# A sequence convolution with expert layers: the first tile of each pass stored whole behind its last addition, in place of two halves of 64 channels

## The chip, the core and the metric

One core of one Trainium2 chip runs the whole program. The metric is the device time of one launch in microseconds (us). Times of engines and transfers come from one execution that the hardware profiler recorded.

## The reference, cut to what matters

```python
# x: (8, 4096, 512) float32; T = 4096 tokens; 8 experts of rank 64, 2 per token
x = x + L0_attn(layernorm(x))      # a convolution along the sequence, for each channel
x = x + L0_ffn(layernorm(x))       # low-rank experts; y is added for the first 4096 rows only

def L0_attn(x, ...):               # 16 decaying states per channel make the kernel k
    ...
    out = irfft(rfft(xt, n=2 * l) * rfft(k, n=2 * l))[..., :l]
    return swapaxes(out) + x * omega
```

Input and output are 64 MiB each. The tokens of sequence 0 are the ones that the experts treat between the two halves of the convolution.

## The kernel before, in words

The 8 sequences are handled in two passes (g = 0 and 1) of four sequences each. A pass holds 128 positions on the partitions and 128 rows (4 sequences x 32 chunks) beside each other, and goes over the 512 channels in DG = 4 tiles of 128 channels. Tiles are numbered t = 0 to 3 in pass 0 and 4 to 7 in pass 1. A tile is computed in BT = 8 blocks of 16 channels, each block in two units of 8 channels, so UT = 16 units per tile. Between the passes the tokens go through the experts.

The buffer `xb` has two halves, each the size of one tile (128 partitions x 128 rows x 128 channels, 8 MiB). Tile t is computed in place in one half: GpSimd (POOL, L625) and VectorE (DVE, L1342) subtract the mean from a unit's 8 channels, DVE multiplies (L1353), TensorE (PE) convolves (L1562, L1575, L1587), and DVE adds the result back into `xb` (L1364), which counts the semaphore `s_ev` up by one per unit. The other half of `xb` is meanwhile emptied of tile t-1 and filled with tile t+1.

All these transfers are issued by the queue of SyncE (SP), in an order written out by hand in `tile(g, t, first, final)`. A tile is moved in PIECES = 16 pieces of PR = 8 rows. A whole piece is 512 KB: 1024 runs of 512 bytes (128 channels). A half piece (`store_part` with 64 channels) is 256 KB: 1024 runs of 256 bytes. In HBM the runs lie 2048 bytes apart. For each of the 8 blocks the queue first issues the tap and decay tables of the block three ahead (`load_weights`, L787 and L791, 256 and 128 KB, which wait for ACT and POOL to be done with the buffers), then some four or five pieces.

What it issues in the pass's tiles (they are called first, second, third and fourth below):

- In the first tile: 16 loads of the second tile into the other half (L732), then, from block 4 on and after `s_ev` has reached half of the tile's units, 16 half stores of the tile itself, channels 0 to 63 (L851, counted by `s_early`).
- In the second tile: a wait until all units of the first are added (`s_ev` >= 16 t); 16 half stores of the first tile's channels 64 to 127 (L851, `s_put[j]`), and 16 loads of the third tile (L732). Load j goes into the rows that store j has emptied and waits for `s_put[j]`. `in_turn` (LAG is 4) orders them: four stores, then load and store by turns (12 of each), then the last four loads.
- In the third tile: the same order, but with 16 whole stores (`store_tile`, L749) and the loads of the fourth tile.
- In the fourth tile: 16 whole stores of the third; then half stores of the fourth's first 64 channels, and the other 64 after its last unit.

DVE and POOL begin a tile only when all of its 16 pieces have landed (`wait(..., s_x, loads_in(...))`). The second tile of a pass is ready long before and its first blocks overlap the last of the first tile (`joined(t)`); at the other borders DVE first makes the last additions of the tile and then takes the next.

```python
            def in_turn(n):
                m = n - LAG
                if not 0 <= m < 2 * (PIECES - LAG):
                    return n
                return LAG + m // 2 if m % 2 else PIECES + m // 2
```

Of the kernel before, what the change touches and what calls it, by code (L numbers as in the profile page):

```python
# [20 lines left out]
P = 128  # L21
# [6 lines left out]
def wait(eng, sem, value):  # L28

    if isinstance(value, int) and value <= 0:  # L30
        return
    eng.wait_ge(sem, value)
# [16 lines left out]
def build(nc, x, delta, alpha, beta, gamma, omega, ew, ei, w1a, w1b, w2a, w2b, out, ei_experts=8):  # L49
# [5 lines left out]
    DG = D // P  # L55
# [3 lines left out]
    UT = P // UC  # L59
# [3 lines left out]
    BT = UT // 2  # L63
# [10 lines left out]
    PIECES = 16  # L74
    PR = P // PIECES
    YP = CH // PR
# [36 lines left out]
    with ctx:  # L113
# [3 lines left out]
        def sem(name):  # L117
            return ctx.enter_context(nc.semaphore(name))
# [172 lines left out]
        s_ev = sem("s_ev")  # L291
        s_early = sem("s_early")
        s_put = [sem(f"s_put{k}") for k in range(PIECES)]
# [140 lines left out]
        def _(pool):  # L434
# [263 lines left out]
                    scatter(q - 2, (q - 2) % 4)  # L698

            pool.wait_ge(s_sf, 4)  # L700
            pool.wait_ge(s_early, 16 * (PIECES + YP))
            for j in range(YP):
                pool.wait_ge(s_put[j], 16 * DG)
            pool.wait_ge(s_yz, 16)
# [15 lines left out]
        def _(sp):  # L720
            def piece(g, t, j, per=PR):

                v = ((t + g) % 2) * P + j * per, g * P + j * per, (t % DG) * P
                return [a if isinstance(a, int) else sp.snap(a) for a in v]

            def load_tile(g, t, pieces, stored=None, per=PR):

                for j in pieces:
                    r0, row, d0 = piece(g, t, j, per)
                    if stored is not None:  # L730
                        wait(sp, s_put[j], 16 * stored(j))
                    sp.dma_start(xb_row[:, bass.ds(r0, per), :], x_rows[:, bass.ds(row, per), bass.ds(d0, P)])\  # L732
                      .then_inc(s_x, 16)
# [3 lines left out]
            def stored(g, t):  # L737

                return lambda j: t + 1 if g == 0 or j < YP else t

            def store_tile(g, t, pieces):

                for j in pieces:
                    r0, row, d0 = piece(g, t, j)
                    if g == 0 and j < YP:
                        dst = y_rows[:, j * PR:(j + 1) * PR, bass.ds(d0, P)]
                    else:
                        dst = o_rows[:, bass.ds(row, PR), bass.ds(d0, P)]
                    sp.dma_start(dst, xb_row[:, bass.ds(r0, PR), :]).then_inc(s_put[j], 16)  # L749
# [27 lines left out]
            def load_weights(i, k):  # L777

                kb = i % NK if isinstance(i, int) else sp.snap(i % NK)
                row = taps_d[bass.ds(kb, 1)].rearrange("k s i d -> k (s i d)")  # L780
                dec = decay_d[bass.ds(kb, 1)].rearrange("k s n d -> (k s) (n d)")
                turned, placed = 2 * (i - WB + 1), i - WB + 1
                now(sp, turned, placed)
                wait(sp, s_rev, turned)

                src = bass.AP(row.tensor, row.offset, [[2, ZR], [2 * (P + ZR), SB], [1, 2 * P]])
                sp.dma_start(taps_in[k * ZR:(k + 1) * ZR], src).then_inc(s_w[k], 16)  # L787
                wait(sp, s_wd, placed)
                if isinstance(i, int) and NK <= i < NK + WB:
                    sp.wait_ge(s_dn, grp(NP))  # L790
                sp.dma_start(dk[:, k, :], dec).then_inc(s_dk[k], 16)  # L791
# [6 lines that stand above are left out]
                return LAG + m // 2 if m % 2 else PIECES + m // 2  # L798

            def tile(g, t, first, final):  # L800
                second = t == g * DG + 1
                for b in range(BT):
                    if not (first and b == 0) and not (final and b + WB > BT):
                        load_weights(t * BT + b + WB - 1, (b + WB - 1) % WB)
                    if b == 0 and not first:
                        wait(sp, s_ev, UT * t)

                    paced = b - 1 if first else b
                    for n in range(2 * PIECES * paced // (BT - 1), 2 * PIECES * (paced + 1) // (BT - 1)):
                        j = n if first or final else in_turn(n)  # L810
                        if first and 0 <= j < PIECES:
                            load_tile(g, t + 1, [j])
                        elif first and b >= BT // 2 and PIECES <= j < 2 * PIECES:
                            if j == PIECES:
                                sp.wait_ge(s_ev, UT * t + UT // 2)
                            store_part(g, t, j - PIECES, slice(0, P // 2), s_early)
                        elif second and 0 <= j < PIECES:
                            store_part(g, t - 1, j, slice(P // 2, P), s_put[j])
                        elif not first and 0 <= j < PIECES:
                            store_tile(g, t - 1, [j])  # L820
                        elif PIECES <= j < 2 * PIECES and not first and not final:
                            if second and j == PIECES:
                                sp.wait_ge(s_early, 16 * (PIECES if g == 0 else 2 * PIECES + YP))
                            load_tile(g, t + 1, [j - PIECES], stored(g, t - 1))
                    if final and g == 0 and b >= BT // 2:
                        if b == BT // 2:
                            for j in range(PIECES):
                                sp.wait_ge(s_put[j], 16 * t)
                            for k in range(SQ):
                                sp.wait_ge(s_scat[k], 16 * (NSEND // SQ))  # L830
                            sp.dma_start(slots_l, slot_d.rearrange("(c p) w -> c p w", p=P)).then_inc(s_slots, 16)
                            sp.dma_start(load1a, w1a.rearrange("(m p) d -> p m d", p=P)).then_inc(s_wl1, 16)
                            for j in range(KC):
                                sp.dma_start(load2a[:, j, :], w2a[j * P:(j + 1) * P, :]).then_inc(s_wl, 16)
                            store_early(g, t, range(YP))
                        elif b < BT - 1:
                            copy_out(b - BT // 2)
                    if final and g == 1 and b == BT - 1:
                        store_early(g, t, range(PIECES))

            def store_early(g, t, pieces):

                sp.wait_ge(s_ev, UT * t + UT // 2)
                for j in pieces:
                    store_part(g, t, j, slice(0, P // 2), s_early)

            def store_part(g, t, j, cols, done):

                r0, row, d0 = piece(g, t, j)
                rows = y_rows[:, j * PR:(j + 1) * PR, :] if g == 0 and j < YP else o_rows[:, row:row + PR, :]  # L850
                sp.dma_start(rows[:, :, d0 + cols.start:d0 + cols.stop], xb_row[:, r0:r0 + PR, cols]).then_inc(done, 16)  # L851

            def copy_out(j):

                rows = slice(j * (T // 4), (j + 1) * (T // 4))
                sp.dma_start(o_tok[rows, 0:(DG - 1) * P], y_d[rows, 0:(DG - 1) * P]).then_inc(s_copy, 16)

            def tiles(g):
                t0 = g * DG
                if g == 0:  # L860
                    for k in range(1, WB):
                        load_weights(k, k)
                tile(g, t0, True, False)
                for t in range(t0 + 1, t0 + DG - 1):
                    tile(g, t, False, False)
                tile(g, t0 + DG - 1, False, True)
# [55 lines left out]
            sp.wait_ge(s_ev, UT * NT)  # L922
            for j in range(PIECES):
                store_part(1, NT - 1, j, slice(P // 2, P), s_put[j])
            sp.wait_ge(s_early, 16 * (YP + 3 * PIECES))
            for k in range(2):
                sp.wait_ge(s_s[2 * k], 16 * ((NQ + 1 - k) // 2))
                sp.wait_ge(s_s[2 * k + 1], 16 * (NP // 2))
# [862 lines left out]
```

## Time and profile before

| | |
|---|---|
| time, median of 3 runs | 1080.95 us (1079.19 to 1082.27) |
| the profiled execution's own time | 1070.18 us |
| its span, first to last instruction | 1068.0 us |
| PE busy | 869.4 us (81%) |
| DVE busy | 816.4 us (76%) |
| ACT busy | 761.4 us (71%) |
| POOL busy | 571.5 us (54%) |
| bytes moved | 286.11 MB, mean 268 GB/s |
| pass 0, first tile to the fourth's last addition | about 117 to 375 us |
| pass 1, the same | about 790 to 1046 us |

The profiled execution ran 10.8 us under the median of the three timed runs and 2.2 us over its span; sums made on the trace are made against 1070.18 and then laid onto 1080.95. Busy shares are means over stages with different limits. DMA shares are the packet times of the 16 DMA engines in a stretch; where transfers overlap within an engine they can exceed 1. A time written beside a transfer on the SP queue is that of its issue: when the queues behind it are full, an issue takes long.

### The profile page before, as it was taken

Reading aid. Unit: us, or ns where it says so; the run is one execution under the profiler, and the core shown is the slowest. Engines: PE = TensorE matmul, PEld = TensorE weight load, DVE = VectorE, ACT = ScalarE, POOL = GpSimd, SP = SyncE. Lnnn points to the kernel's source line nnn. Section 1 sums busy time; section 2 is a strip of 40 time slices with the busy share of each in tenths; the row PEclk is TensorE's granted clock in tenths of the full one; section 3 lists DMA queues with packets and bytes.
Section 4 is the critical chain, followed back from the end, with each engine's and each line's share of the span. In section 5 each row is a group of like instructions: output and inputs, shape, how many; then the busy total and the mean of one; then the engine's idle time right before and its main releaser. Section 6 shows DMA issues by size and latency. Waiting matters only on the chain.

```text
span 1068.0 us, 31991 instructions
## 1 busy us (share of the span) xinstructions
PE 869.4 (81%) x11186; PEld 730.9 (68%) x11186; DVE 816.4 (76%) x1350; ACT 761.4 (71%) x1124; POOL 571.5 (54%) x641
## 2 busy tenths in 40 slices
PE   2770588887868969999999999997878889786981
PEld 1550477776757758888888888886757777675771
DVE  7988899987969834577777777775689998797891
ACT  3882599997969756566665665664459999696990
POOL 5444788867857232666666656655553333332330
PEclk9995699998989979999999999999989999898996
DMA  8999899999999979999999999899669999999977
GB/s 300 351 400 385 211 264 209 271 266 295 308 279 285 327 182 309 257 293 318 286 312 259 242 268 244 246 256 240 174 157 268 226 252 281 287 296 300 295 159 158
DMA packets 390529, 286.11 MB, mean 268 GB/s; under 512 B 124784, under 2 KB 338434, under 8 KB 389948
## 3 DMA queue, kind: packets, MB, share of 16 engines
q1 hardware_dynamic: 345980, 211.67, 72.6%
q0 software_dynamic: 17952, 34.42, 14.6%
q10 hardware_dynamic: 26528, 39.14, 10.4%
q8 instruction: 39, 0.64, 0.3%
q14 instruction: 30, 0.25, 0.1%
HBM read 195.57 MB, written 98.77 MB: 276 GB/s over the span
## 4 chain that ended last, share of the span: by engine, by line
PE 31%; issue 17%; ACT 15%; DVE 14%; DMA 13%; POOL 3%; SPq 2%; DVEq 1%; ACTq 1%; POOLq 0%
PE ps L1688 8%; DMA xb<-L_attn_x 6%; PE ps L1714 6%; ACT wb L1032 6%; DVE xb L1364 4%; ACT wb L1038 4%; PE ps L1562 4%; PE ps L1575 3%; PE ps L1587 3%; DMA wide<-y_d,slot_g 3%; ACT carry L1008 3%; DVE wb L1182 2%; PE ps L1650 2%; PE ps L1663 2%; DVE state L1380 2%
## 5 line engine op out<-in xcount | busy, mean ns | idle before, releaser
L1575 PE MATMUL ps<-xn,wb 128*128 128x128 f32 x2048 | 273.0, 288 | 0.0
L1575 PEld LDWEIGHTS ps<-xn,wb 128*128 128x128 f32 x2048 | 248.0, 198 | 17.0 <-issue 2.3
L625 POOL TENSOR_TENSOR cen<-xb,mean 128x512 f32<-128x512 f32 x128 | 142.8, 1119 | 217.0 <-DVE state L1380 144.2
L1353 DVE TENSOR_TENSOR xn<-cen,rstd 128x1024 f32<-128x1024 f32 x128 | 177.1, 1384 | 44.9 <-POOL cen L625 36.1
L1140 ACT ACTIVATE cen<-ps 128x1024 f32<-128x1024 f32 x110 | 109.2, 1023 | 101.6 <-PE ps L1688 64.7
L1562 PE MATMUL ps<-xn,near 128*32 128x128 f32 x2048 | 87.5, 291 | 113.0 <-DVE xn L1353 67.9
L1364 DVE TENSOR_TENSOR xb<-xb,ps 128x1024 f32 (+1 forms) x128 | 152.7, 1193 | 7.6 <-PE ps L1587 7.6
L1031 ACT ACTIVATE wb<-wide 32x1024 f32<-32x1024 f32 x126 | 144.5, 1147 | 15.4 <-DMA wide<-taps_d 12.9
L1562 PEld LDWEIGHTS ps<-xn,near 128*32 128x32 f32 x2048 | 52.6, 113 | 137.2 <-issue 72.1
L1688 PE MATMUL ps<-carry,wb 64*128 64x256 f32 x1024 | 126.8, 388 | 7.7 <-DVE carry L1426 4.6
L1688 PEld LDWEIGHTS ps<-carry,wb 64*128 64x128 f32 x1024 | 99.4, 190 | 37.1 <-issue 18.5
L1195 DVE BATCH_NORM_STATS2 xb<-xb 128x512 f32 (+1 forms) x128 | 84.3, 684 | 45.3 <-DMA xb<-L_attn_x 45.1
L1032 ACT ACTIVATE wb<-wide 32x768 f32<-32x768 f32 x126 | 114.8, 911 | 1.5
L505 POOL DMA_INDIRECT slot_d<-rowf,posi x64 | 106.1, 1658 | 11.9 <-issue 11.9
L1342 DVE TENSOR_TENSOR cen<-xb,mean 128x512 f32<-128x512 f32 x128 | 90.2, 705 | 9.3 <-DMA xb<-L_attn_x 9.2
L1714 PE MATMUL ps<-cen,xn 128*64 128x128 f32 x1536 | 96.4, 275 | 0.0
L1587 PE MATMUL ps<-state,carry 32*128 32x128 f32 x2048 | 93.6, 297 | 0.0
L1182 DVE BATCH_NORM_STATS2 wb<-xb 128x512 f32 (+1 forms) x128 | 79.8, 681 | 15.7 <-DMA xb<-L_attn_x 14.5
L1714 PEld LDWEIGHTS ps<-cen,xn 128*64 128x64 f32 x1536 | 84.3, 137 | 5.3 <-issue 5.1
L1587 PEld LDWEIGHTS ps<-state,carry 32*128 32x128 f32 x2048 | 69.2, 186 | 25.9 <-issue 25.1
L1038 ACT ACTIVATE wb<-wb 64x512 f32<-64x512 f32 x128 | 80.5, 629 | 4.9 <-DVE wb L1466 1.8
L1008 ACT ACTIVATE carry<-far,rate 128x384 f32<-128x384 f32 x128 | 79.0, 617 | 3.2
(211 smaller groups left out, 1311.4 us busy)
## 6 DMA issues: line engine op xcount, KB each, us to landing
xb<-L_attn_x SPq DMA_DIRECT2D x160, 512.0 KB, 7.4
out<-xb SPq DMA_DIRECT2D x72, 512.0 KB, 6.4
xb<-L_attn_x ACTq DMA_DIRECT2D x128, 256.0 KB, 5.8
out<-xb SPq DMA_DIRECT2D x88, 256.0 KB, 4.7
wb<-L_ffn_w_B SPq DMA_DIRECT2D x78, 256.0 KB
wide<-taps_d SPq DMA_DIRECT2D x63, 256.0 KB, 5.8
dk<-decay_d SPq DMA_DIRECT2D x63, 128.0 KB, 5.6
out<-y_d SPq DMA_DIRECT2D x4, 1536.0 KB, 11.6
```

The source lines that it names most:

```text
L625: pool.tensor_tensor(cen[:, k, 0:QB // 2].rearrange("p b r d -> p r b d"), unit_view(pool, g, i, k)[:, :, 0:UC // 2] .rearrange("p r (b d) ...
L1008: act.activation(carry[:, k, 0:CR + P], far[:], ACT.Exp, scale=rate[:, bass.ds(col, 1)])\
L1031: act.activation(dst[0:ZR], src, ACT.Copy)
L1032: act.activation(dst[ZR:2 * ZR, :, :, ZR:P], src[:, :, :, 0:P - ZR], ACT.Copy).then_inc(s_rev, 1)
L1038: act.activation(taps[2 * ZR:P, :, :, 2 * ZR:P], taps[0:2 * ZR, :, :, 0:2 * ZR], ACT.Copy)\
L1353: dve.tensor_tensor(xn[:, k].rearrange("p (b d) r -> p b d r", d=2), cen[:, k].rearrange("p b r d -> p b d r"), rstd[:, g * P:(g + 1) * P] ...
L1364: dve.tensor_tensor(view, view, ps[:, QB * k:QB * k + QB, 0:2 * P] .rearrange("p b (d r) -> p r b d", d=2), ALU.add).then_inc(s_ev, 1)
L1562: ins = pe.matmul(ps[b * 2 * N:(b + 1) * 2 * N, QB * k, 2 * P:3 * P], near[:, h, k * QB + b, d:d + 2, :].rearrange("p z n -> p (z n)"), xn ...
L1575: ins = pe.matmul(ps[:, QB * k + b, d * P:(d + 1) * P], wb[:, h, k * QB + b, d, :], xn[:, k, 2 * b + d, :], start=(b > 0 and d == 0), stop ...
L1587: ins = pe.matmul(ps[:, QB * k + b, d * P:(d + 1) * P], carry[rows, k, d * P:(d + 1) * P], state[rows, k, :], start=False, stop=True, skip ...
L1688: ins = pe.matmul(ps[:, 2 * (b % 2) + h, f * QT:(f + 1) * QT].rearrange("p (a t) -> p a t", a=2), w1bs[half_rows, k, c * P:(c + 1) * P], r ...
L1714: ins = pe.matmul(ps[h * RANK:(h + 1) * RANK, 4, 0:P], w2as[:, (f // 2) * (FC // 2) + 2 * b + f % 2, :], act_at(q, b)[:, f, side * P:(side ...
```

## The change

The first tile of a pass is no longer stored in two halves. Its 16 half stores in its own second half are dropped; in the second tile of the pass `store_tile` stores it whole, piece by piece, in the places of the order that the second halves had. The two waits that belonged to the early halves go, and the counts of `s_early` elsewhere follow. Loads, their order, all computation and the third and fourth tiles of each pass stay.

```diff
-            pool.wait_ge(s_early, 16 * (PIECES + YP))
+            pool.wait_ge(s_early, 16 * YP)
...
             def tile(g, t, first, final):
-                second = t == g * DG + 1
...
                         if first and 0 <= j < PIECES:
                             load_tile(g, t + 1, [j])
-                        elif first and b >= BT // 2 and PIECES <= j < 2 * PIECES:
-                            if j == PIECES:
-                                sp.wait_ge(s_ev, UT * t + UT // 2)
-                            store_part(g, t, j - PIECES, slice(0, P // 2), s_early)
-                        elif second and 0 <= j < PIECES:
-                            store_part(g, t - 1, j, slice(P // 2, P), s_put[j])
                         elif not first and 0 <= j < PIECES:
                             store_tile(g, t - 1, [j])
                         elif PIECES <= j < 2 * PIECES and not first and not final:
-                            if second and j == PIECES:
-                                sp.wait_ge(s_early, 16 * (PIECES if g == 0 else 2 * PIECES + YP))
                             load_tile(g, t + 1, [j - PIECES], stored(g, t - 1))
...
-            sp.wait_ge(s_early, 16 * (YP + 3 * PIECES))
+            sp.wait_ge(s_early, 16 * (YP + PIECES))
```

## Rows read from the trace of the kernel before

**Rows 1.** The page's strip of DMA busy tenths in 40 slices.
```profile
DMA  8999899999999979999999999899669999999977
```
**Rows 2.** Timeline at the border from second to third tile, both passes: start, us, instruction, [idle].
```profile
238.26 1.22 DVE L1364 TENSOR_TENSOR xb<-xb,ps 128x1024 f32<-128x1024 f32 x1 [1.28 <-PE ps L1587]
...
242.30 1.59 POOL L625 TENSOR_TENSOR cen<-xb,mean 128x512 f32<-128x512 f32 x1 [9.67 <-DMA xb<-L_attn_x]
...
913.29 2.65 POOL L625 TENSOR_TENSOR cen<-xb,mean 128x512 f32<-128x512 f32 x2 [9.41 <-DMA xb<-L_attn_x]
```
**Rows 3.** Timeline of SP's queue in the second tile, passes 0 and 1: start, us, issues.
```profile
182.39 2.92 SPq L851 DMA_DIRECT2D y_d<-xb  x4
...
187.79 0.42 SPq L732 DMA_DIRECT2D xb<-L_attn_x  x1
...
229.32 6.67 SPq L732 DMA_DIRECT2D xb<-L_attn_x  x4
...
238.94 0.45 SPq L791 DMA_DIRECT2D dk<-decay_d  x1
...
855.02 2.94 SPq L851 DMA_DIRECT2D out<-xb  x4
...
860.34 0.40 SPq L732 DMA_DIRECT2D xb<-L_attn_x  x1
...
900.13 5.99 SPq L732 DMA_DIRECT2D xb<-L_attn_x  x4
...
909.51 1.64 SPq L791 DMA_DIRECT2D dk<-decay_d  x1
```
**Rows 4.** The same timeline in the third tile, passes 0 and 1.
```profile
249.06 0.45 SPq L732 DMA_DIRECT2D xb<-L_attn_x  x1
...
294.52 8.04 SPq L732 DMA_DIRECT2D xb<-L_attn_x  x4
...
911.90 5.39 SPq L749 DMA_DIRECT2D out<-xb  x4
...
919.76 0.48 SPq L732 DMA_DIRECT2D xb<-L_attn_x  x1
...
966.27 7.13 SPq L732 DMA_DIRECT2D xb<-L_attn_x  x4
```
**Rows 5.** DMA view of four stretches: 182:236, 239:302, 855:905 and 912:972.
```profile
DMA packets 33957, 13.83 MB, mean 256 GB/s; under 512 B 17496, under 2 KB 33956, under 8 KB 33956
...
DMA packets 35150, 19.00 MB, mean 302 GB/s; under 512 B 1221, under 2 KB 35147, under 8 KB 35147
...
DMA packets 32755, 13.43 MB, mean 269 GB/s; under 512 B 17038, under 2 KB 32754, under 8 KB 32754
...
DMA packets 33091, 18.00 MB, mean 300 GB/s; under 512 B 693, under 2 KB 33089, under 8 KB 33089
```
**Rows 6.** Timeline of SP's queue: the stores in the first tile, and in the fourth.
```profile
152.80 3.35 SPq L851 DMA_DIRECT2D y_d<-xb  x2
...
177.97 0.67 SPq L791 DMA_DIRECT2D dk<-decay_d  x1
...
307.32 6.29 SPq L749 DMA_DIRECT2D y_d<-xb  x4
...
340.24 0.82 SPq L791 DMA_DIRECT2D dk<-decay_d  x1
```
**Rows 7.** Timeline of DVE: the eighth and the sixteenth addition of pass 0's first tile.
```profile
151.58 1.18 DVE L1364 TENSOR_TENSOR xb<-xb,ps 128x1024 f32 x1
...
181.18 1.19 DVE L1364 TENSOR_TENSOR xb<-xb,ps 128x1024 f32<-128x1024 f32 x1
```
**Rows 8.** Waits in 117:182 (total, times, longest us); then the chain: start, us, what.
```profile
PE ps L1562 <- DVE xn L1353: 38.6, 1, 38.6
...
119.81 3.71 PE ps L1575 x16
...
246.44 3.71 PE ps L1575 x16
```

## The prediction, as put on record before the changed kernel ran

> **What bounds the kernel now.** I read the page's strips first. The DMA engines are busy nine tenths or more in nearly every slice [rows 1], so it is not enough to ask which engine computes longest; one has to ask at each border between tiles whether the data or the computation comes last. The view that answers this is the timeline around a border. At the end of the second tile of pass 0, DVE makes its last addition from 238.26 to 239.48 us and could take the next tile at once; POOL had been idle for 9.67 us and begins the third tile at 242.30, released by a load of `x`. In pass 1 it is the same, at 913.29 after 9.41 us [rows 2]. So the third tile starts when the last of its 16 pieces lands, in both passes. The reader should see that a microsecond more in the transfers ahead of this point moves everything behind it by a microsecond.
>
> Next the timeline of SP's queue in that stretch, to see what sets the landing. The second tile's stream begins at 182.39 with the first half store (the last addition of the first tile has just come in) and its last four loads are issued from 229.32 to 235.99: 53.6 us for 16 half stores, 16 loads and the tables. In pass 1 it goes from 855.02 to 906.12, 51.1 us [rows 3]. Four issues take 2.9 us at the start, four loads 6 to 6.7 us at the end: the queues are full by then and the issue waits for the DMA engines. The stream is bound by the transfers, not by the order's waits.
>
> **What is removed from the first tile: nothing on the path.** 16 half stores per pass go from the second half of the first tile. What the computation could gain there is bounded by the pitch of the additions. From the eighth to the sixteenth, 151.58 to 181.18, eight units take 29.6 us, 3.70 each, with the half stores running [rows 7]. From there to the last addition of the second tile, 238.26, are 16 units in 57.1 us, 3.57 each, the last two of them short because no next unit is staged between them [rows 2, 7]. Even if the whole difference were owed to the stores it would be 8 x 0.13 = 1.0 us. I take 0. The dropped work can't be used for anything else there: the second tile is already loaded and the third needs the rows that the first still occupies. The wait for `s_early` at the first load of the second tile goes too; by the rows those halves were issued by 178 us, and the load behind that wait was issued at 187.79 [rows 3, 6], so it cost nothing. The waits at the pass's end cost nothing either, as they count stores from 200 us earlier. No computing instruction is added, and the number of packets falls.
>
> **What is added to the second tile: 16 x 256 KB = 4.19 MB per pass, ahead of the last load.** In each of the 16 places a whole store stands where a half stood. The trace has the whole form next door, in the third tile, in the same order with the same neighbours. Four ways to price 16 whole in place of 16 half stores:
>
> 1. The alternating part alone, 12 loads and 12 stores with five pairs of tables. Pass 0: 229.32 - 187.79 = 41.5 us with halves, 294.52 - 249.06 = 45.5 whole, so 3.9 us for 12 and 5.2 for 16. Pass 1: 900.13 - 860.34 = 39.8 and 966.27 - 919.76 = 46.5, so 6.7 for 12 and 9.0 for 16 [rows 3, 4].
> 2. Bytes over rate. In pass 0 the second tile moves 13.83 MB at 256 GB/s in 54 us and the third runs at 302 GB/s. With 4.19 MB more and that rate: 18.02 / 0.302 = 59.7 us, so 5.7 more. In pass 1: 17.62 MB at 300 GB/s is 58.7 us against 50, so 8.7 more [rows 5].
> 3. Stores without loads beside them, each with four pairs of tables. The first tile's 16 halves run from 152.80 to 178.64, 25.8 us; the fourth tile's 16 whole from 307.32 to 341.06, 33.7 us. Difference 7.9 [rows 6].
> 4. The whole stream, from first store to last load issued. Pass 1: 51.1 us in the second tile, 973.4 - 911.90 = 61.5 in the third, so 10.4 more [rows 3, 4]. This is too much by the backlog that the third tile inherits: its first four stores take 5.39 us to issue where the second tile's take 2.94, because the loads before them are still under way, while the second tile starts with empty queues. I keep it as the upper end.
>
> The values lie between 5.2 and 10.4 us. For pass 0 I take 7, between the 5.2 to 5.7 of its own rows and the 7.9 of the store-only rows; for pass 1, where its own rows say 8.7 and 9.0, I take 8.5.
>
> The Trainium skill (DMA: Bandwidth & Descriptors, Specifications) asks for 512 bytes or more per run for line rate and says that below that the engine does a read-modify-write. It would favour this change, which turns 256-byte runs into 512-byte ones. The trace agrees only in part: a half store is dearer than half a whole one, but not as dear as a whole one.
>
> **Whether anything absorbs it.** In pass 0 the tables behind the loads are issued by 239.39 and the third tile's first store goes out at 239.51, just when the last addition of the second tile (239.48) allows it [rows 2, 3]. With the stream 7 us later, SP comes to that wait 7 us after it is met, so the third tile's stream is late by the same amount as its computation. In pass 1 SP was done at 911.15 and waited 0.75 us for the last addition [rows 3, 4]; that wait disappears, so I give back 0.5. The third tile ends in the same race, which the loads won't win better than before, since both sides moved together. The fourth has nothing to load, its computation sets its end, and it starts later by the whole delay. PE's clock: PE waits longer at the border, and the first group behind such a wait costs 3.71 us at the lower clock; but it costs 3.71 us behind the 38.6 us of idle time at the pass's start as well as behind the present gap [rows 8], so a longer gap adds nothing. What is late next is thus the start of the third tile, the fourth, the experts behind pass 0, and the end.
>
> **Sum.** 0 from the first tile, +7.0 in pass 0, +8.5 - 0.5 in pass 1: +15.0 us. The profiled execution took 1070.18 us, so its like would take 1085.2. The profiled execution is 10.8 us below the median of the timed runs; the delay doesn't depend on what makes that difference, so I add it to the median: 1080.95 + 15 = 1096 us.
>
> **Rivals.**
> A, the delay is as long as the third tile's stream says, 10.4 in each pass, because the first loads now also wait for whole stores to land. For it: the order is the third tile's to the letter. Against it: the queues are empty at 182 and 855 us. +20.8 us: 1102.
> B, no change. By the skill's rule on runs under 512 bytes, taken to the letter, a half store would cost the DMA engines as much as a whole one; as a mechanism of this kernel, the time would go by runs and not by bytes. For it: both streams have about the same number of packets (33,957 and 35,150, 32,755 and 33,091) [rows 5]. Against it: the times for them differ, 25.8 against 33.7 us in the store-only stretches [rows 6]. It gives 0: 1081.
> C, faster. The short runs are what slows the loads beside them, and whole stores let the loads go so much quicker that the stream becomes shorter. The rate does rise, from 256 to 302 and from 269 to 300 GB/s. The point that decides: the rate must reach 18.02 MB / 54 us = 334 GB/s in pass 0 and 17.62 / 50 = 352 in pass 1 for no loss; no stretch of the third tile holds more than 302 on the mean [rows 5]. If the stream then came early enough to end the loads at the last addition, it would save the 242.30 - 239.48 = 2.8 us of pass 0 and, in pass 1, the about 1.4 us from the last addition (SP's first store of 911.90 shows it) to 913.29: 1080.95 - 4.2 = 1077 [rows 2, 4]. The 1 us of the first tile, in two passes 2, would add to it.
> D, half the delay: the cheap 5.2 us of pass 0 in both passes and the 1 us gain of the first tile twice: +8.4, 1089.
>
> **How the numbers follow.** My forecast, 1096 with its own span of 1092 to 1100, has 0.66; A 0.10, D 0.13, B 0.07, C 0.04. The range reaches from D to A, 1089 to 1102, and leaves B, C and a little beyond A outside. A measurement of this kernel can tell about 0.3% from no change, 3.2 us. Forecast, A and D are slower by more: 0.89; B is the same, 0.07; C is faster, 0.04.
>
> **What the profile after would show.** Right: no stores on SP's queue in the first tile, the additions there still 3.7 us apart; in the second tile L749 in place of L851, the last four loads issued up to some 243 us in pass 0 and 59 to 60 us after the stream's start in pass 1; POOL's wait for the load at that border 16 to 18 us in place of 9.7 and 9.4; a rate of about 300 GB/s there; and the third and fourth tiles as long as before. Wrong: a rate near 340 GB/s in the second tile (towards B or C), a pitch in the first tile under 3.6 us, or a third tile that gains back what the second lost. A pass 0 with much less delay than pass 1 would mean that the alternating part, my first price, was the right one by itself.

## The result and the profile after

The changed kernel takes 1092.09 us (median of 4 runs, 1088.57 to 1095.47) against 1080.33 us for the kernel before (4 runs, 1079.19 to 1082.27). The ratio is 1.0119, with a 95% interval of 1.0090 to 1.0148: 1.2% slower. The profiled execution spans 1089.6 us, its own time is 1091.77.

The page's summary and the totals of the DMA engines, after:

```profile
span 1089.6 us, 31957 instructions
...
DMA  8999994999999989999999999999679299999976
...
DMA packets 357249, 286.11 MB, mean 263 GB/s; under 512 B 58736, under 2 KB 305154, under 8 KB 356668
```

The same 286.11 MB now travel in 33,280 packets fewer (the page before had 390,529), and two dips (the 4 and the 2) have come into the DMA strip where it had nines [rows 1]. They are the second halves of the two first tiles, which have lost their stores. The DMA engines have less to do in all, and the kernel is slower.

The timeline of SP's queue in pass 0's and pass 1's second tile (start, us, issues) answers to [rows 3]:

```profile
181.47 3.91 SPq L749 DMA_DIRECT2D y_d<-xb  x4
...
188.69 0.65 SPq L732 DMA_DIRECT2D xb<-L_attn_x  x1
...
234.61 7.45 SPq L732 DMA_DIRECT2D xb<-L_attn_x  x4
...
245.25 7.96 SPq L749 DMA_DIRECT2D y_d<-xb  x4
...
868.96 3.98 SPq L749 DMA_DIRECT2D out<-xb  x4
...
921.67 7.59 SPq L732 DMA_DIRECT2D xb<-L_attn_x  x4
```

From the first store to the last issued load it is now 242.06 - 181.47 = 60.6 us in pass 0 (53.6 before) and 929.26 - 868.96 = 60.3 in pass 1 (51.1 before). What comes of it is seen at the border to the third tile, the point at which the third tile's last load has landed and POOL begins to compute it. The timelines of DVE and POOL answer to [rows 2]:

```profile
237.38 1.22 DVE L1355 TENSOR_TENSOR xb<-xb,ps 128x1024 f32<-128x1024 f32 x1 [1.21 <-PE ps L1578]
248.41 0.69 DVE L1333 TENSOR_TENSOR cen<-xb,mean 128x512 f32<-128x512 f32 x1 [9.81 <-DMA xb<-L_attn_x]
...
248.47 1.59 POOL L625 TENSOR_TENSOR cen<-xb,mean 128x512 f32<-128x512 f32 x1 [16.72 <-DMA xb<-L_attn_x]
...
935.95 2.65 POOL L625 TENSOR_TENSOR cen<-xb,mean 128x512 f32<-128x512 f32 x2 [18.10 <-DMA xb<-L_attn_x]
```

POOL waits 16.72 and 18.10 us where it waited 9.67 and 9.41: 7.1 and 8.7 us more, and for the same loads. The DMA view of 181:242 and 869:929 shows the added bytes and the rate, beside [rows 5]:

```profile
DMA packets 33923, 18.02 MB, mean 295 GB/s; under 512 B 1109, under 2 KB 33921, under 8 KB 33921
DMA packets 33514, 18.03 MB, mean 301 GB/s; under 512 B 662, under 2 KB 33511, under 8 KB 33511
```

The second tile now looks like the third did: its packets are as many as before, its bytes 18.0 in place of 13.8 and 13.4 MB, and the rate 295 to 301 GB/s. The first tile has not become quicker. Its eighth and its sixteenth addition, beside [rows 7]:

```profile
150.65 1.19 DVE L1355 TENSOR_TENSOR xb<-xb,ps 128x1024 f32 x1
...
180.26 1.19 DVE L1355 TENSOR_TENSOR xb<-xb,ps 128x1024 f32<-128x1024 f32 x1
```

29.6 us for eight units, as before.

**Where the 21.6 us between the two profiles are.** The spans differ by more than the medians (11.8 us), so I divide them at DVE's first multiplication of a pass and the end of its last addition. Pass 0 takes 257.6 us before and 263.8 after, pass 1 257.1 and 264.7: +6.2 and +7.6, together 13.7. Between the passes, where the two kernels do the same, the experts take 414.8 us before and 423.6 after, +8.8; start and end make -0.9. The experts' stretch is 413 to 430 us long among all executions profiled here. On one chip it took 423.2 us in the changed kernel (e8) and 415.8 and 416.2 in two kernels with the same late stores (e9, e10), so I take its 8.8 us for scatter. That the change has no part in it is not shown. For everything below, the lengths of the two passes are therefore read beside the times.

### The profile page after: what moved, and what is told of

Same layout as the page of the kernel before. It is cut to its first block, busy times and chain, and to the rows that moved or that the text cites. A ratio compares the mean times of both kernels' runs of the same rounds, so it can differ in the third digit from the quotient of the medians.

```text
span 1089.6 us, 31957 instructions
## 1 busy us (share of the span) xinstructions
PE 875.3 (80%) x11186; PEld 731.7 (67%) x11186; DVE 813.4 (75%) x1350; ACT 761.7 (70%) x1124; POOL 570.6 (52%) x641
## 2 busy tenths in 40 slices
DMA packets 357249, 286.11 MB, mean 263 GB/s; under 512 B 58736, under 2 KB 305154, under 8 KB 356668
## 4 chain that ended last, share of the span: by engine, by line
PE 37%; issue 16%; ACT 14%; DVE 12%; DMA 8%; SPq 6%; POOL 2%; ACTq 1%; DVEq 1%; POOLq 0%
PE ps L1679 10%; PE ps L1705 10%; ACT wb L1023 5%; DMA xb<-L_attn_x 4%; ACT wb L1029 4%; DVE xb L1355 4%; PE ps L1654 3%; PE ps L1641 3%; PE ps L1553 3%; SPq L732 3%; DVE wb L1173 2%; ACT carry L999 2%; PE ps L1721 2%; SPq L749 2%; PE ps L1578 2%
## 5 line engine op out<-in xcount | busy, mean ns | idle before, releaser
L1566 PE MATMUL ps<-xn,wb 128*128 128x128 f32 x2048 | 271.7, 288 | 0.0
L1566 PEld LDWEIGHTS ps<-xn,wb 128*128 128x128 f32 x2048 | 247.0, 197 | 17.0 <-issue 2.3
L1131 ACT ACTIVATE cen<-ps 128x1024 f32<-128x1024 f32 x110 | 109.5, 1024 | 93.4 <-PE ps L1679 53.7
L505 POOL DMA_INDIRECT slot_d<-rowf,posi x64 | 106.3, 1661 | 11.8 <-issue 11.7
L1705 PE MATMUL ps<-cen,xn 128*64 128x128 f32 x1536 | 99.2, 275 | 0.0
L1705 PEld LDWEIGHTS ps<-cen,xn 128*64 128x64 f32 x1536 | 86.8, 137 | 5.7 <-issue 5.7
L1003 ACT ACTIVATE shift_s<-ps,coef 128x124 f32<-128x124 f32 x128 | 45.5, 356 | 63.2 <-PE ps L1553 62.2
```

The source lines that it names most:

```text
L1131: act.activation(act_at(q, b).rearrange("p f t -> p (f t)"), ps[:, 2 * (b % 2):2 * (b % 2) + 2, :].rearrange("p a t -> p (a t)"), ACT.Gelu ...
L1566: ins = pe.matmul(ps[:, QB * k + b, d * P:(d + 1) * P], wb[:, h, k * QB + b, d, :], xn[:, k, 2 * b + d, :], start=(b > 0 and d == 0), stop ...
L1705: ins = pe.matmul(ps[h * RANK:(h + 1) * RANK, 4, 0:P], w2as[:, (f // 2) * (FC // 2) + 2 * b + f % 2, :], act_at(q, b)[:, f, side * P:(side ...
```

## The experiments

Each time is compared with the kernel before on the same chip (medians there: 1072.4 us for e1 to e4, 1083.6 for e5 to e7, 1073.8 for e8 to e10). "Stream" is the span on SP's queue from the first late store to the last issued load of the second tile; a "whole" store is a transfer of 128 channels, a "half" of 64; "pass" runs from DVE's first multiplication to the end of its last addition. Streams and passes are read from one profiled execution for each kernel, the ratio from all timed ones.

| kernel | late stores per pass 0 / 1 | stream, us | passes, us | ratio (95%) |
|---|---|---|---|---|
| before | 16 halves / 16 halves | 53.6 / 51.1 | 257.6 / 257.1 | 1 |
| changed | 16 whole / 16 whole | 60.6 / 60.3 | 263.8 / 264.7 | 1.0119 (1.0090 to 1.0148) |
| e1 | whole / halves | 61.6 / 53.3 | 264.0 / 256.4 | 1.0083 (1.0051 to 1.0115) |
| e2 | halves / whole | 53.9 / 60.3 | 258.2 / 268.5 | 1.0077 (1.0049 to 1.0105) |
| e3 | whole, early halves kept | 61.4 / 60.7 | 265.7 / 263.0 | 1.0150 (1.0111 to 1.0189) |
| e4 | halves, early ones dropped | 53.9 / 51.7 | 258.4 / 255.3 | 1.0011 (0.9975 to 1.0047) |
| e5 | 96 channels | 57.8 / 56.6 | 264.7 / 258.5 | 1.0073 (1.0044 to 1.0101) |
| e6 | 32 halves | 72.1 / 69.0 | 276.6 / 273.5 | 1.0301 (1.0269 to 1.0333) |
| e7 | 48 channels, early 80 | 50.8 / 51.5 | 260.1 / 260.3 | 1.0083 (1.0054 to 1.0113) |
| e8 | the changed kernel again | 60.8 / 61.3 | 265.6 / 266.2 | 1.0153 (1.0110 to 1.0197) |
| e9 | whole, eight stores ahead | 61.9 / 62.5 | 267.3 / 264.6 | 1.0158 (1.0122 to 1.0194) |
| e10 | e3 again | 60.7 / 60.8 | 265.0 / 263.0 | 1.0128 (1.0086 to 1.0170) |

### e1 and e2: one pass at a time

```diff
-                        elif first and b >= BT // 2 and PIECES <= j < 2 * PIECES:
+                        elif g == 1 and first and b >= BT // 2 and PIECES <= j < 2 * PIECES:
...
-                        elif second and 0 <= j < PIECES:
+                        elif g == 1 and second and 0 <= j < PIECES:
```

(and `g == 0` for e2; the waits on `s_early` follow.)

> Whole stores in pass 0 alone, pass 1 as before. Theory (4.19 MB more ahead of the last load of the third tile, per pass, each pass paying for itself): pass 0 from its first xn to its last addition takes 263.8 us as in the changed kernel (257.6 before), pass 1 stays at 257.1, the time is about 6 us over before's, ratio 1.005 to 1.006. Rival (the delay arises between the passes or by a hand-over from pass 0 to pass 1): pass 1 is longer too, or the time moves by all of 12 us or by nothing.

> Whole stores in pass 1 alone, pass 0 as before. Theory: pass 0 stays at 257.6 us, pass 1 takes 264.7 us as in the changed kernel, the time is about 7.5 us over before's, ratio 1.007; with the run of pass 0 alone it adds up to the whole change. Rival: the two don't add up, because one of the passes hides what the other pays.

Only the altered pass grew: 264.0 and 256.4 us in e1, 258.2 and 268.5 in e2. The 268.5 is 3.8 us more than was expected, and 2 of these arose before any late store: the stream begins 67.5 us into that pass, where it begins 65.4 us into the changed kernel's. Why is open; the stream itself has the length of the others. SP's queue in e2 shows both kinds of stream in one execution, pass 0 with halves and pass 1 with whole stores:

```profile
182.64 2.92 SPq L851 DMA_DIRECT2D y_d<-xb  x4
...
229.72 6.86 SPq L732 DMA_DIRECT2D xb<-L_attn_x  x4
...
860.57 3.99 SPq L749 DMA_DIRECT2D out<-xb  x4
...
912.81 8.10 SPq L732 DMA_DIRECT2D xb<-L_attn_x  x4
```

The times rose by 0.83% and 0.77%, each interval holding what was expected (0.55 and 0.7%). Together they make 1.6%, and the whole change 1.2 and, in e8, 1.5%: within the intervals they add up, and nothing shows that one pass hides what the other pays.

### e3, e10 and e4: are the first tile's stores free?

e3 (and e10, the same kernel) keeps the early halves and stores the tile whole on top:

```diff
                         elif second and 0 <= j < PIECES:
-                            store_part(g, t - 1, j, slice(P // 2, P), s_put[j])
+                            if j == 0:
+                                sp.wait_ge(s_early, 16 * (PIECES if g == 0 else 2 * PIECES + YP))
+                            store_tile(g, t - 1, [j])
...
```

e4 keeps the late halves and drops 28 of the 32 early ones, so that these channels of the first tiles are not in its output:

```diff
-                        elif first and b >= BT // 2 and PIECES <= j < 2 * PIECES:
+                        elif first and g == 0 and b >= BT // 2 and PIECES <= j < PIECES + YP:
...
```

> The 16 early half stores stay in the first tile of each pass, and the second tile stores the tile whole on top (the first 64 channels are written twice, with the same values). Theory (the first tile's stores lie beside its computation and cost nothing): time and both passes as in the changed kernel, about 1092 us, 263.8 and 264.7 us. Rival (dropping the early stores gave up to 1 us back per pass, so that the second tile's cost is larger than it looks): 1 to 2 us above the changed kernel.

> As before, but the early half stores of the first tile are left out (28 of the 32; the four that the experts read stay), so the first 64 channels of most of the first tiles are not in the output. Theory: 28 transfers fewer and no gain: the passes take 257 to 258 us and the time is before's within 0.2%. Rival (the first tile's stores slow its computation, or leave a backlog that the second tile's stream inherits): 1 to 4 us faster than before.

> The kernel with early halves and whole stores on top once more, now beside the changed kernel on the same chip. Theory: the same time as the changed kernel, ratio between the two within 0.3%. Rival: 2 to 4 us slower, because the early stores cost the first tile something that the change gives back.

With the early stores back in, the time is 1086.18 us, and in e10 1086.96 beside 1091.43 for the changed kernel on the same chip, where the ratios to before are 1.0128 and 1.0153 with intervals that overlap. The two are 0.4% apart where 0.3 was expected, which six executions of each don't tell from nothing, and the rival wanted e10 the slower by 2 to 4 us; it isn't. Without them and with nothing added late, the time is 1072.67 us against 1072.39. So 8.4 MB (e3) or 7.3 MB (e4) in the second half of the two first tiles cost nothing that can be seen, in either direction. The times alone would miss some 4 us (e4's interval is 0.36% to either side); the border is finer and says the same: POOL's wait in pass 0 is 17.14 us in e3 and 10.73 in e4 (timeline of POOL; e3 first, then e4):

```profile
249.33 1.59 POOL L625 TENSOR_TENSOR cen<-xb,mean 128x512 f32<-128x512 f32 x1 [17.14 <-DMA xb<-L_attn_x]
```

```profile
242.86 1.59 POOL L625 TENSOR_TENSOR cen<-xb,mean 128x512 f32<-128x512 f32 x1 [10.73 <-DMA xb<-L_attn_x]
```

In pass 1 it is 18.93 and 8.96. The wait goes with what is stored late and takes no notice of the early halves.

### e5 and e6: bytes and runs

e5 splits the tile at 32 channels; e6 issues each late whole store as two halves, with a semaphore of its own for the first.

```diff
-                            store_part(g, t, j - PIECES, slice(0, P // 2), s_early)
+                            store_part(g, t, j - PIECES, slice(0, P // 4), s_early)
...
-                            store_part(g, t - 1, j, slice(P // 2, P), s_put[j])
+                            store_part(g, t - 1, j, slice(P // 4, P), s_put[j])
```

```diff
                         elif second and 0 <= j < PIECES:
+                            store_part(g, t - 1, j, slice(0, P // 2), s_h[j])
                             store_part(g, t - 1, j, slice(P // 2, P), s_put[j])
...
+                            if second:
+                                sp.wait_ge(s_h[j - PIECES], 16 * (g + 1))
                             load_tile(g, t + 1, [j - PIECES], stored(g, t - 1))
```

> Half the dose: 32 channels stored early (runs of 128 bytes), 96 late (384 bytes). The number of late stores and runs is that of before and of the changed kernel, only the bytes are between. Theory (a late store costs some 0.7 us for its 1024 runs plus 0.5 us for each 256 KB): the second tile's stream is 3.5 to 4.5 us longer than before's, the passes take about 261 us, the time is about 6 us over before's. Rival (only runs under 512 bytes are dear, because of something done at that threshold): 384-byte runs cost as much as 512-byte ones or more, so the whole 12 us or more.

> The changed kernel, with each late whole store issued as two half stores one after the other: the same bytes in the same place, but 32 transfers of 256-byte runs in place of 16 of 512-byte runs. It splits the change into its two parts, the move and the merging of runs. Theory: a half costs some 1.2 us of the DMA engines, a whole 1.7, so the second tile's stream is 16 x 0.7 = 11 us longer than the changed kernel's in each pass and the time about 20 us over it, near 1112. Rival (the time goes by bytes): the same as the changed kernel, 1092.

In e5 the stream is 57.8 and 56.6 us long, halfway between halves (mean of the six such streams in the table: 52.9) and whole stores (mean of the ten four-ahead streams: 60.9), and the time is 0.73% up, about 8 us where 6 were expected. Its passes are unlike, 264.7 and 258.5 us where about 261 was expected for each, but the difference lies behind the border: from the start of the pass to POOL's start at the border they take 129.0 and 128.6 us, between the 125.1 and 123.7 of the kernel before and the 132.3 and 132.4 of the changed one. The rival with a threshold at 512 bytes wanted 12 us or more for the time and is out. In e6 the stream is 72.1 and 69.0 us and the kernel 3.0% slower than before, about 16 us over the changed one by the ratio of e8 and 20 by the first result's, where 20 were expected. SP's queue and the DMA view of 182:254 in e6, pass 0:

```profile
182.30 7.90 SPq L851 DMA_DIRECT2D y_d<-xb  x8
...
247.79 6.65 SPq L735 DMA_DIRECT2D xb<-L_attn_x  x4
```

```profile
DMA packets 49966, 17.72 MB, mean 246 GB/s; under 512 B 34128, under 2 KB 49964, under 8 KB 49964
```

About the same bytes as in the changed kernel in 16,000 packets more, at 246 in place of 295 GB/s. The DMA engines are full in all these stretches: their share is 1.04 and 1.07 in e6's two streams, 1.08 and 1.09 in the changed kernel's, 1.02 and 1.08 in those before, so it is they and not SP's issuing that set the length. That gives both terms of a late store. 16 more transfers of 1024 runs each, with the bytes unchanged, cost 70.6 - 60.9 = 9.7 us (70.6 is the mean of e6's two streams), 0.61 us for a transfer and its 1024 runs. As e6 doubles transfers and runs together, no run here tells what the transfer costs by itself. 256 KB more in each of 16 transfers, with the runs unchanged, cost 60.9 - 52.9 = 8.0 us, 0.50 us for each 256 KB. So the change is made of two parts that oppose each other: the move of 16 halves behind the last addition, 70.6 - 52.9 = 17.7 us per pass, and the merging of two halves into one whole store, which gives 9.7 back. At 32 late transfers a second thing is late as well: POOL waits for a decay table, and DVE's last additions of the second tile slip from 239 to 247 us (timeline of POOL, e6):

```profile
238.87 0.60 POOL L575 COPY near<-dk 128x256 f32<-128x256 f32 x1 [4.33 <-DMA dk<-decay_d]
```

### e7: more of the tile stored early

```diff
-                                sp.wait_ge(s_ev, UT * t + UT // 2)
-                            store_part(g, t, j - PIECES, slice(0, P // 2), s_early)
+                                sp.wait_ge(s_ev, UT * t + 10)
+                            store_part(g, t, j - PIECES, slice(0, 80), s_early)
...
-                            store_part(g, t - 1, j, slice(P // 2, P), s_put[j])
+                            store_part(g, t - 1, j, slice(80, P), s_put[j])
```

> The other direction: 80 channels early (runs of 320 bytes, issued once 10 of the 16 units are added), 48 late (192 bytes). Theory: 1 MB less ahead of the last load takes 16 x 0.125 = 2 us off the second tile's stream, but the early stores, begun 7.4 us later and longer, end some 10 us later and run into its start, so that most of it is lost: passes 256 to 259 us, the time 2 us under to 3 us over before's. Rival (bytes behind the last addition are all that counts): POOL's wait at the border shrinks by 2 us in each pass and the time falls by 4 us.

Here 80 channels are stored early and 48 late. The stream became shorter, 50.8 and 51.5 us, 1.7 on the mean, as the price by bytes said. But it begins later. SP's queue in e7, pass 0, from the last early stores on:

```profile
177.44 6.64 SPq L851 DMA_DIRECT2D out<-xb  x5
184.12 1.40 SPq L787 DMA_DIRECT2D wide<-taps_d  x1
185.57 0.45 SPq L791 DMA_DIRECT2D dk<-decay_d  x1
186.06 4.42 SPq L851 DMA_DIRECT2D y_d<-xb  x4
...
230.37 6.53 SPq L732 DMA_DIRECT2D xb<-L_attn_x  x4
```

The first late store goes out at 186.06 in place of 182.39 [rows 3], and with a queue that is not empty: four issues take 4.42 us for fewer bytes than took 2.92. POOL's wait at the border is 12.31 us in place of 9.67, and in pass 1 14.92 in place of 9.41. The expectation that 2 us would be gained and mostly lost was too kind: the time is 0.83% up (5.8 to 12 us), more than the 3 us allowed. The passes show 2.5 and 3.2 us over those of before (260.1 and 260.3 against 257.6 and 257.1). They account for 5.7 of the about 9 us. At the border the delay is already 2.6 and 5.6 us (127.7 and 129.2 us from the start of the pass, against 125.1 and 123.7), 8.2 together; behind it pass 1 took 2.4 us less than before, which is within the scatter of that stretch (129.8 to 133.8 us over the ten passes with whole stores). What is shown is that the split at 64 channels is not improved by moving it to 80.

### e8 and e9: the changed kernel again, and a longer lead

```diff
...
-                        j = n if first or final else in_turn(n)
+                        j = n if first or final else in_turn(n, 2 * LAG if t == g * DG + 1 else LAG)
```

> The changed kernel itself, once more, on the same chip as the runs sent with it, to see how far single executions scatter and to compare the others with it directly. Theory: ratio to before 1.012 to 1.016, passes 263 to 267 us, the second tile's stream (first late store to last load issued) 60 to 61.5 us.

> The changed kernel with eight stores instead of four ahead of the first load in the second tile of each pass (the third tile keeps four). Theory (the stream is bound by the DMA engines and not by loads that wait for stores to land): stream, border and time as in the changed kernel within 1 us per pass. Rival A of the prediction (loads wait for whole stores to land): the wait vanishes with the longer lead, the stream gets 2 to 3 us shorter per pass and the time falls by 5 us.

e8 repeats the result in another set of executions at 1.0153 (1.0110 to 1.0197), with passes of 265.6 and 266.2 us. With eight stores ahead the first loads have twice the time to see their rows stored; the stream is 61.9 and 62.5 us, 1.1 us longer than in e8, and the ratio is 1.0158. Nothing is gained, and the changed kernel's own waits say why. In its second tile of pass 0 SP's queue waits for the last addition and for ACT, but never for a store to land (waits of SP, 181:243; total, times, longest us):

```profile
SPq L749 <- DVE xb L1355: 10.5, 1, 10.5
SPq L787 <- ACT wb L1023: 1.0, 2, 0.7
```

Rival A's mechanism falls. The border to the third tile in e9 (timeline of POOL):

```profile
250.94 1.59 POOL L625 TENSOR_TENSOR cen<-xb,mean 128x512 f32<-128x512 f32 x1 [18.29 <-DMA xb<-L_attn_x]
```

## Why the prediction was right

1096 us (1089 to 1102) was forecast, 1092.1 was measured, a delay of 11.8 us where 15.0 was written; e8 repeats it at 1.53% (1.10 to 1.97), 16 us, and the passes' own lengths say 13.7 in the first pair of profiles. The 11.8 us alone would not decide between the forecast and rival D, which wanted 8.4; the passes, the streams and e8 do. Over all profiles, ten passes with whole stores last 264.9 us on the mean and the six with halves 257.2: 7.8 us per pass and 15.6 for two.

- **The first tile gives nothing back: right.** Eight units took 29.6 us with and without the stores, and e3, e4 and e10 show no price for them. Rival D's 1 us per pass falls.
- **The whole stores cost 7 us in pass 0 and 8.5 in pass 1: right as a sum.** The streams grew by 7.0 and 9.2 us, the waits at the border by 7.1 and 8.7. The price by bytes and rate (5.7 and 8.7) was low in pass 0 and right in pass 1, and that by stores alone (7.9) comes closest to the 7.8 us over all passes; the one from the third tile's whole stream (10.4) was too high, and the alternating part of pass 0 alone (5.2) too low. Half a late store is 0.50 us for 256 KB over all streams, 8.0 us for 16.
- **Nothing behind absorbs it: nearly right.** From POOL's start at the border to the end of the pass it took 131.5 us in place of 132.5 in pass 0 and 132.2 in place of 133.4 in pass 1, so 1.1 and 1.2 us came back where 0 and 0.5 were written. The third tile's part of it, from POOL's start there to POOL's start of the fourth, is 66.4 against 67.5 us in pass 0 and 67.7 against 68.0 in pass 1. Over the ten passes with whole stores the stretch behind the border is 129.8 to 133.8 us long, so that anything is absorbed is not shown.
- **The clock: a longer wait costs no more, as was written.** At the border of pass 0 the granted clock is 0.50 (the 1.2 GHz level) before and after, and from PE's first group of the third tile to its second group of L1575 (L1566 after) it takes 6.2 us before and 6.3 after. At the border of pass 1 the clock came back to 1.00 sooner in the changed kernel, and the same step took 5.3 us in place of 6.5; this single pair would be the change's gain, but over all runs it is 5.3 to 6.5 us with halves and 5.3 to 6.6 with whole stores, so it is scatter. The chain at the border of pass 1, before:

```profile
918.16 3.71 PE ps L1575 x16
```

and after, at the start of pass 0 and at the border of pass 1:

```profile
118.73 3.71 PE ps L1566 x16
...
940.82 3.10 PE ps L1566 x16
```

- **Rival B, time by runs alone,** is out by e5, where the runs were the same and the time was not. The Trainium skill's rule on 512 bytes (DMA: Bandwidth & Descriptors, Specifications) reads like a threshold. It names no price; that a half store would cost as much as a whole one was my reading of it. Across late stores of 192, 256, 384 and 512 bytes per run the streams here take 51.2, 52.9, 57.2 and 60.9 us, a line in which no step at 512 can be seen (the 51.2 of e7 start behind a queue that is not empty). Had the fixed cost been due below 512 bytes only, the means of the other streams (52.9, 60.9 and 70.6 us) would put e5's at about 59.3 us, an estimate: 9.7 us over 32 halves is 0.30 us each, the rest of a half is 0.80 us for 256 KB, and 16 x (0.30 + 1.5 x 0.80) = 24.0 us stand in place of 17.7. Its two are 57.8 and 56.6. The Trainium skill (DMA: Bandwidth & Descriptors, Why small descriptors are slow) speaks of a fixed cost for each packet, and this fits in kind: 0.61 us for a transfer and its 1024 runs beside 0.50 for their 256 KB. By those numbers the fixed part is 55% of a half store, more than the 27% that the Trainium skill gives there for the first of two fixed costs at 256 bytes. The 55% holds the cost of the transfer too, so the two are not quite the same thing; for this kernel the measurement decides.
- **Rival C, faster,** needed 334 and 352 GB/s in the second tile; it had 295 and 301.

The term that stays the least certain is the whole effect on the time itself, because the experts' stretch scatters by more than a pass gains or loses: 1.2% in one set, 1.5% in the other, 1.6% as the sum of e1 and e2. The three agree within their intervals.

## What to carry to other kernels

Ask of a transfer not only what it costs the DMA engines but in front of which landing it stands: here 33,280 packets were saved in all and 1.2% lost, because the bytes went from a stretch in which no landing was waited for into the one that a tile's start waits for. Early is free only while it ends early: in e7 the early stores ran into the late ones, and both borders came later. A stretch next door that already has the new form is the best price list, read three ways (the alternating part, bytes over rate, stores alone) and not by its whole length, which carries the backlog that it inherited. When single executions scatter, cut the trace at fixed instructions and compare the parts that the change touches.

## What the runs showed that was not expected

The price of a late store looked like a line and not like a step: about 0.61 us for a transfer of 1024 runs and 0.50 us per 256 KB, so merging 32 halves into 16 whole stores in one place is worth 9.7 us, more than the 8.0 us by which the changed kernel's stream is longer. And the same kernel's executions differ by up to 16 us on one chip (1065 to 1081 us for the kernel before, 28 runs). In the profiles the largest differences outside the change lie in the experts' stretch: 423.2 us in e8 and 415.8 in e9 on one chip, 413 to 419 in e1 to e4 on another, 429 to 430 in e5, e6 and e7 on a third, where the kernel before also takes 1083.6 us in place of 1072.4 and 1073.8. So part of it goes with the chip. Why it differs was not tried.
